# First layer of a two-layer cross-attention: a head's output is turned and summed one step later

## The reference

```python
q = split(x @ Wq.T); k = split(ctx[:, :77] @ Wk.T); v = split(ctx[:, :77] @ Wv.T)
k_ip = split(ctx[:, 77:] @ Wk_ip.T); v_ip = split(ctx[:, 77:] @ Wv_ip.T)
out = softmax(q @ k.T / 4) @ v + softmax(q @ k_ip.T / 4) @ v_ip
x = merge(out) @ Wo.T + bo + x
```

## Time and profile before

| what | value |
|---|---|
| median of 3 runs | 1654.46 us (1651.66 to 1658.3) |
| the profiled execution: its time | 1653.78 us |
| the profiled execution: its span | 1651.9 us |
| PE busy over the span | 1556.8 us, 94% |
| DVE busy | 1274.3 us, 77% |
| ACT busy | 1093.0 us, 66% |
| POOL busy | 558.9 us, 34% |
| chain that ended last, by engine | PE 75%, DVE 10%, ACT 9%, issue 3%, SPq 2%, DMA 2% |

### The profile page before, as it was taken

How to read it: one execution, slowest core, us unless ns; L and a number is a source line. 1 busy time by engine, 2 the same in 40 slices (tenths; PEclk the granted TensorE clock), 3 DMA queues, 4 the chain that set the end, 5 groups by cost and what they waited for, 6 DMA issues and landing times.

```text
span 1651.9 us, 25857 instructions
## 1 busy us (share of the span) xinstructions
PE 1556.8 (94%) x7936; PEld 1182.3 (72%) x7936; DVE 1274.3 (77%) x3548; ACT 1093.0 (66%) x2319; POOL 558.9 (34%) x1313
## 2 busy tenths in 40 slices
PE   6899999999999899999999989999999999999993
PEld 3565489999556459999756538999965654899981
DVE  3698378987789549999769936888887983799975
ACT  1597378885389448888439926888826973788860
POOL 0343044443044224444115403444403430444430
PEclk9899999999999999999999999999999999999995
DMA  9110310010411230000221131000030113000100
GB/s 319 40 43 18 105 62 21 20 36 1 125 35 44 65 104 20 20 26 26 76 59 40 46 105 53 25 20 21 22 125 20 45 32 105 20 20 20 36 1 16
DMA packets 67536, 84.15 MB, mean 51 GB/s; under 512 B 29236, under 2 KB 38212, under 8 KB 67400
## 3 DMA queue, kind: packets, MB, share of 16 engines
q1 hardware_dynamic: 64728, 77.38, 15.9%
q10 hardware_dynamic: 2672, 5.13, 0.9%
HBM read 41.75 MB, written 34.10 MB: 46 GB/s over the span
## 4 chain that ended last, share of the span: by engine, by line
PE 75%; DVE 10%; ACT 9%; issue 3%; SPq 2%; DMA 2%; POOL 0%; POOLq 0%; ACTq 0%; DVEq 0%
PE ps_w L1024 42%; PE ps_s L1024 14%; PE ps_t L1024 11%; PE ps_b L1024 5%; DVE probsT_low L776 3%; ACT probs L592 3%; ACT probsT_high L573 2%; ACT probsT L581 2%; DVE row_max L839 2%; PE ps_b L1158 2%; DVE probs L863 1%; DVE stat L848 1%; ACT probs L607 1%; PE ps_m L1024 1%; DMA slots<-out_all 1%
## 5 line engine op out<-in xcount | busy, mean ns | idle before, releaser
L573 ACT ACTIVATE probsT_high<-ps_t 128x512 fp32r<-128x512 f32 x640 | 385.0, 602 | 90.5 <-PE ps_t L1024 90.4
L776 DVE TENSOR_TENSOR probsT_low<-probsT,probsT_high 128x512 fp32r<-128x512 f32 x560 | 379.3, 687 | 17.5 <-ACT probsT L581 12.4
L581 ACT ACTIVATE probsT<-ps_t 128x512 f32<-128x512 f32 x640 | 387.9, 606 | 0.0
L1024 PE MATMUL ps_w<-gram,probsT_high 128*128 128x416 f32 (+2 forms) x1280 | 383.1, 310 | 0.0
L1024 PE MATMUL ps_w<-gram_low,probsT_high 128*128 128x384 f32 (+2 forms) x1280 | 352.0, 304 | 0.0
L500 POOL TENSOR_SCALAR exp_bias<-row_max 128x1 f32<-128x1 f32 x320 | 137.1, 429 | 536.2 <-DVE row_max L839 536.2
L607 ACT ACTIVATE probs<-ps_s,exp_bias 128x508 f32<-128x508 f32 x320 | 220.8, 691 | 130.0 <-POOL exp_bias L500 89.1
L1024 PE MATMUL ps_s<-slots 96*128 96x512 f32 x640 | 280.7, 481 | 22.8 <-DVE row_max L791 9.3
L1024 PE MATMUL ps_t<-slots 98*128 98x512 f32 x640 | 251.8, 413 | 1.2 <-DMA slots<-row_max 0.2
L1024 PEld LDWEIGHTS ps_w<-gram_low,probsT_high 128*128 128x128 f32 (+1 forms) x1280 | 242.0, 189 | 6.5
L1024 PE MATMUL ps_w<-gram,probsT_low 128*128 128x400 f32 (+2 forms) x1280 | 246.1, 314 | 0.0
(11 more groups left out here) (170 smaller groups left out, 2014.1 us busy)
## 6 DMA issues: line engine op xcount, KB each, us to landing
slots<-parts SPq DMA_DIRECT2D x128, 192.0 KB, 3.3
parts<-probsT_high SPq DMA_DIRECT2D x16, 512.0 KB, 4.2
parts<-probsT_high SPq DMA_DIRECT2D x24, 256.0 KB, 4.0
parts<-probsT_low SPq DMA_DIRECT2D x8, 512.0 KB, 3.6
parts<-x_sb SPq DMA_DIRECT2D x8, 512.0 KB, 3.9
slots<-probsT_high SPq DMA_DIRECT2D x24, 128.0 KB, 3.3
parts<-probsT_low SPq DMA_DIRECT2D x12, 256.0 KB, 3.7
ctx_sb<-in_ctxT ACTq DMA_DIRECT2D x3, 1024.0 KB, 5.5
```

The costliest lines, as they stand in the source:

```text
L573: nc.scalar.activation(probsT_high[1 - par][:, t, :], ps_t[:, t % 2, :], ACT.Exp, scale=SCALE)
L581: nc.scalar.activation(probsT[:, t, :], ps_t[:, t % 2, :], ACT.Exp, scale=SCALE).then_inc(pt_block[l], 1)
L776: nc.vector.tensor_tensor(probsT_low[1 - par][:, t, :], probsT[:, t, :], probsT_high[1 - par][:, t, :].bitcast(F32), ALU.subtract).then_in ...
L1024: return nc.tensor.matmul(out, lhsT, rhs, start=start, stop=stop)
```

## The change

TensorE's four transposes of head n leave the end of step n. They become `output_turned`, called for head n-1 in step n, between transposed block 1 and `values_low(0)`. VectorE's sum leaves its place between the first-half maxima and the low part of block 2 of step n, and is done for head n-1 in step n, between the second-half maxima and the low part of block 3. Head 19's transposes and sum follow `run_heads0`. The semaphore values are the same, and no instruction is added or taken away.

```diff
@@ VectorE, step0 @@
+            def output_summed(b, n):
+                dve.wait_ge(o_done, HEADS * b + n + 1)
+                nc.vector.tensor_reduce(out=o0_all[:, n, :, :],
+                                        in_=ps_b[:, 0:SC * V0S].rearrange("p (c a w) -> p c w a", c=SC, a=2),
+                                        axis=AX.X, op=ALU.add).then_inc(o_moved, 1)
                 if scores:
                     maxima0(b, n + 2, 1, par)
+                if use and n > 0:
+                    output_summed(b, n - 1)
                 if use:
                     lowT(b, 0, n - 1, 1 - par, 3)
...
                     output(last, 2)
-                if use:
-                    dve.wait_ge(o_done, HEADS * b + n + 1)
-                    nc.vector.tensor_reduce(...).then_inc(o_moved, 1)
                 if transposed:
                     lowT(b, 0, n, par, 2)
@@ VectorE, batch @@
                 run_heads0(step0, dve, b)
+                output_summed(b, HEADS - 1)
@@ TensorE, step0 @@
                     by_channels(last, "y", "o1", heads_outT, (1,))
+                if use and n > 0:
+                    output_turned(b, n - 1)
                 if use:
                     values_low(0)
                     values_low(1)
...
-                if use:
-                    pe.wait_ge(oT_moved, g + 1 + CREDIT)
-                    pe.wait_ge(o_moved, g + CREDIT)
-                    pe.sem_inc(passed, 1)
-                    (four transposes of outT0[par]) .then_inc(o_done, 1)
+            def output_turned(b, n):
+                head = HEADS * b + n
+                pe.wait_ge(oT_moved, head + 1 + CREDIT)
+                pe.wait_ge(o_moved, head + CREDIT)
+                pe.sem_inc(passed, 1)
+                for c in range(SC):
+                    last = nc.tensor.transpose(ps_b[:, V0S * c:V0S * c + V0S], outT0[n % 2][:, P * c:P * c + P],
+                                               ident[0:V0S, 0:V0S])
+                last.then_inc(o_done, 1)
@@ TensorE, batch @@
                 run_heads0(step0, pe, b)
+                output_turned(b, HEADS - 1)
```

More of the change, by code:

```diff
@@ L818, in step0 @@
                     output(last, 2)
-                if use:
-                    dve.wait_ge(o_done, HEADS * b + n + 1)
-                    nc.vector.tensor_reduce(out=o0_all[:, n, :, :],
-                                            in_=ps_b[:, 0:SC * V0S].rearrange("p (c a w) -> p c w a", c=SC, a=2),
-                                            axis=AX.X, op=ALU.add).then_inc(o_moved, 1)
                 if transposed:
```

## The result

The changed kernel takes 1697.82 us (median of 4 runs, 1696.95 to 1700.14) against 1654.46 us before (4 runs, 1651.66 to 1658.3): a ratio of 1.0263, 95% interval 1.024 to 1.0286, so 43 us slower. The forecast was 1700.5. The changed kernel's profiled execution has a span of 1695.2 us, 43.3 more than before.

A forecast was written before the change was run, and what follows sets the result against it. No engine full; of two tied loops it followed scores and maxima between TensorE and VectorE. 4 x (9.8 + 1.8) = 46 us on 1653.78 gave 1700, with 0.7 for the median 1700.5; range 1686 to 1712, chance 0.84.

The forecast's parts named there:

- The mechanism: In VectorE's step the moved sum waits 0.5 us for the transposes; maxima queued behind it make TensorE's scores late.
- The step: Steps 1 to 16 of each batch: 5.58 us in place of 4.97, 0.61 more; spacing of sums 5.5 to 5.6.
- maxima's end to scores: Semaphore's way from VectorE's maxima to TensorE's next scores, taken as 0.11 us.
- my low bound: Semaphore's way from maxima to scores at 0.05 us instead of 0.11: 5.52 us a step, 0.55 more.
- The idle time before the sum: VectorE, each of 64 steps: about 0.5 us idle before the sum, released by the transposes.
- The last steps: Steps 17 to 19, set by ScalarE, and the last head: copies late by 0.90 us twice, 1.8 us a batch.
- outside the stage: Step 0, between the layers and loads behind this stage: no cost, priced at 0.
- That the sum never waits: Transposes end before VectorE has the maxima: step 5.08, 11 us more, 1665 us; chance 0.08 including what lies toward the forecast.
- That the copy's leaving makes the step shorter: Copy leaves the chain, step falls at least to VectorE's own 4.61 us: 23 us faster, 1632; chance 0.03.
- The clock held at 1.00 in the stage: Judges the case that TensorE's idle time lowers its clock: 95 us more, 1795 if it lasted; chance 0.05.
- the old place was nearly free: Sum and transposes before the change lay in gaps where TensorE waits for maxima; removing the transposes is worth next to nothing.

The follow-up runs named there:

- Both halves alone: Two runs against the changed kernel: VectorE's sum put back at its old place, 1654.89 us; TensorE's transposes put back at the step's end, 1656.74 us.
- the sum's place alone: Changed kernel with TensorE's transposes put back at the end of their own step, only VectorE's sum moved: 1656.74 us, ratio 1.0029.
- TensorE's half alone: Changed kernel with VectorE's sum put back behind the first-half maxima, only the transposes moved: 1654.89 us, ratio 1.0012.

## Why the prediction was right

- **The mechanism** was as described: the sum waits for the transposes in each step, TensorE then waits for the maxima, VectorE's lines 776, 790, 791 came into the chain and the copy left it. Both halves alone and the edit that only moves the transposes forward show that neither order by itself makes the 43 us.
- **The step** came out at 5.44 us, where the working gave 5.58 and named 5.5 to 5.6 as the sign. By its terms: transposes start at 2.08 instead of 2.12 and take 0.41 instead of 0.44; sum at 2.53 instead of 2.59; it occupies 0.35 instead of 0.38; the two low parts 1.20 instead of 1.22; maxima's end to scores 0.06 (112.45 to 112.51) instead of 0.11. That last one, 0.05, is the largest: 0.11 was read at the first-half scores, and the loop goes over the second-half ones, where the earlier trace rows had shown 0.05, my low bound. I took 0.11 as measured with TensorE waiting, which was misread: value products ran on it until 107.63 + 0.64 = 108.27, past the weight load at 108.12. The second-half maxima started 0.89 us after the scores (107.98), as worked out. The idle time before the sum reads 0.34 us and not 0.5: the profile counts from the end of the maxima (109.27), my 2.09 from the moment at which the next instruction could be issued; in my way of counting it was 2.53 - 2.09 = 0.44.
- **The last steps** cost a little more than forecast. From the second-half scores of step 1 to the last sum, the second batch took 92.54 us before (463.92 to 556.46) and takes 102.36 (478.50 to 580.86): 9.8 more, 11.6 forecast. 16 steps of 0.48 are 7.7, so the last steps carry 2.1, where I had 1.8.
- **The remainder.** The four batches give 10.0, 9.8, 10.1 and 10.5, together 40.4 of the 43.3 us. The other 2.9 come from outside the stage, which I had priced at 0: 2.8 more up to step 1 of the first batch, 1.7 more from the first batch's last sum to step 1 of the second, 0.2 less over the next two such stretches and 1.5 less behind the last sum. The granted clock differed there between the two profiled executions. The filling steps, timeline of before in its second and third batch, then of after in its second, and after's window:

```profile
447.73 2.93 PE L1024 MATMUL ps_b<-probs,w_o 128*128 128x512 f32 x6
...
845.42 4.56 PE L1024 MATMUL ps_b<-probs,w_o 128*128 128x512 f32 x6
```

```profile
460.70 4.54 PE L1028 MATMUL ps_b<-probs,w_o 128*128 128x512 f32 x6
```

```profile
461.00:465.00 4.00, 4.00 (x6) 1.00 (x5) 1.23 (x2) 0.00 (x0) 0.00 (x0) 0.63 0.04 1
```

- The same six matmuls took 1.6 us longer at a mean clock of 0.63. The change isn't needed for that: the kernel before has 2.93, 4.56 and 4.34 us for them in its second, third and fourth batch, the changed one 4.54, 4.58 and 2.93. The last projections went the other way: from VectorE's last long instruction of the batch to the end of the span, 1629.9 to 1651.9 before and 1677.6 to 1695.2 after, 21.9 against 17.6 us, and in the other ten profiles between 19.5 and 22.2. Where the 2.8 us of the first batch come from stays open.
- **How much of the hit was luck.** The forecast added 46 us and 43.3 were measured, but the terms were not that good. The step was priced 0.13 us too high, 8 us over 64 steps. The last steps, priced at 7.2 us in all, cost 9.7, and the stretches outside the stage added 2.9; both made up for part of it. The stage alone would have given 1654.46 + 40.4 = 1695, inside the range still.
- **The rivals.** That the sum never waits (1665 us) is nearest to the run with the sum's place alone: a step of 5.05, for which the working gave 5.08. That the two agree is in part chance, since its loop would have given 4.95 with the times of that run, and a loop over ScalarE, which the working left out, gives the rest. The time was 1656.74. That the copy's leaving makes the step shorter didn't come: with TensorE's half alone the copy was out of TensorE's way and the step stayed at 4.96. The clock held at 1.00 in the stage, with TensorE idle for 0.9 us in each step. The swing that the Trainium skill describes for short idle times in a cycle over the banks (TensorE: Matmul & The Clock Gate, A second HAM failure mode: psum-queue depth-cycling) didn't show in this stage.
- **Not quite right** was the argument that the old place was nearly free. The sum and transposes lay in a gap, but without slack: doubled transposes cost their full time there.
- **One more thing that wasn't seen ahead**: in the order of before, VectorE's low part of block 2 starts as ScalarE's exponentials end (in the run with TensorE's half alone it waits 0.35 us for them). So a third loop, over ScalarE, ties as well: in the run with TensorE's half alone the chain goes from the copy over the exponentials of block 2 to that low part and the maxima. Taking the copy out of it alone brought nothing either, since the loop over block 0 is as long. In the changed kernel the low part waits for ScalarE too (107.37, 0.34 us) and the maxima behind it start at 107.98, just as the scores' end allows: there the loop over ScalarE costs nothing, and it is the one that comes next once the wait of the sum is gone.

## What to carry to other kernels

When two in-order engines feed each other twice in a step, add up each closed way over both queues, in-order work between the waits included; the longest sets the step (it may pass a third engine and close only after two steps), and an instruction moved to hide a wait must not land on one. Putting a consumer one step later helps only if its producer is also ahead of it in the other engine's queue. Where several loops are nearly of one length, single edits show nothing, and a common edit that leaves one engine full shows the gain of all.

## What the runs showed of the hardware

- With TensorE's half alone and ScalarE's copy last, 15 of the 49 low parts between 70 and 150 us take 715 to 849 ns, and none of the others over 694. Beside each of the 15 GpSimd runs its second instruction of L471 (the values' low part, 128 rows of four blocks of 16 columns, 0.30 us), for 0.16 us beside the one of 715 and 0.30 beside the one of 849; between these a low part takes longer by about as much as the two run together. The instruction's line in that kernel, and in the kernel with TensorE's half alone, where none takes over 693:

```profile
L776 DVE TENSOR_TENSOR probsT_low<-probsT,probsT_high x49: 681/693/849, 69.9 to 149.3; 128x512 fp32r<-128x512 f32 x49
```

```profile
L776 DVE TENSOR_TENSOR probsT_low<-probsT,probsT_high x49: 674/683/693, 69.7 to 149.8; 128x512 fp32r<-128x512 f32 x49
```

- The time from the maxima's end to the next scores' weight load isn't one number: 0.11 us at the first-half scores, behind value products; 0.06 at the second-half scores, behind transposes (0.05) as well as where TensorE had stood idle for 0.9 us (0.06). Which of its conditions makes the difference no run here shows.
